# Eight to ten spare bf16 matmuls behind each matrix-vector product of a Householder tridiagonalisation

## The reference

```python
deg = jnp.sum(A, axis=0) + jnp.sum(A, axis=1) - jnp.diagonal(A)
L_norm = d_inv_sqrt[:, None] * (jnp.diag(deg) - A) * d_inv_sqrt[None, :]
_, U = jnp.linalg.eigh(L_norm)
agg = jnp.einsum('mn,bnd->bmd', U.T, features)
h = jax.nn.relu(agg @ W1 + b1)
return jnp.einsum('nm,bmd->bnd', U, h @ W2 + b2)
```

## Time and profile before

| | |
|---|---|
| median of 3 runs | 9881.85 us (9870.64 to 9885.23) |
| profiled execution | 9871.62 us, of it the span of the trace 9869.9 us |
| PE matmul busy | 5128.9 us, 52% |
| VectorE busy | 7105.6 us, 72% |
| ScalarE, GpSimd busy | 18%, 12% |
| steps of the tridiagonalisation | 1022 (x1022 at L483) |
| mean granted TensorE clock | 0.71 of full speed |

### The profile page before, as it was taken

How to read it: one execution, slowest core, us unless ns; L and a number is a source line. 1 busy time by engine, 2 the same in 40 slices (tenths; PEclk the granted TensorE clock), 3 DMA queues, 4 the chain that set the end, 5 groups by cost and what they waited for, 6 DMA issues and landing times. The chain is left out here.

```text
span 9869.9 us, 311313 instructions
## 1 busy us (share of the span) xinstructions
PE 5128.9 (52%) x128994; PEld 3544.3 (36%) x128994; DVE 7105.6 (72%) x33446; ACT 1777.0 (18%) x4691; POOL 1178.6 (12%) x5177
## 2 busy tenths in 40 slices
PE   5675878777777767766654433121111110047856
PEld 2354555555555555554443332010000000033355
DVE  3555666767777776777777778989898989954154
ACT  1432111111111111111111121121111110011054
POOL 0000111111222221222222221000000000000000
PEclk8898999999999777555555555555555555579988
DMA  1000000000000000000000000000000000000000
GB/s 35 1 0 18 4 4 4 4 4 4 4 4 4 4 4 3 4 4 4 4 3 3 3 3 2 0 0 0 0 0 0 0 0 0 0 0 1 17 0 17
DMA packets 24537, 40.99 MB, mean 4 GB/s; under 512 B 2464, under 2 KB 20128, under 8 KB 23200
## 3 DMA queue, kind: packets, MB, share of 16 engines
q1 hardware_dynamic: 23200, 21.70, 0.7%
HBM read 17.50 MB, written 4.19 MB: 2 GB/s over the span
## 5 line engine op out<-in xcount | busy, mean ns | idle before, releaser
L289 PE MATMUL tri_y<-L 128*32 128x256 f32 (+7 forms) x36792 | 2091.7, 366 | 11.9 <-issue 11.6
L289 PEld LDWEIGHTS tri_y<-L 128*32 128x32 f32 x36792 | 1282.2, 132 | 250.7 <-issue 47.9
L1338 PE MATMUL ev_agree<-ev_prod,ev_fold 128*128 128x448 bf16 x520 | 241.5, 568 | 1683.3 <-DVE ev_prod L1461 1666.7
L272 PE MATMUL tri_k<-tri_kp,tri_half 128*32 128x1 f32 x8176 | 270.0, 191 | 1329.4 <-DVE tri_x L472 1329.4
L272 PEld LDWEIGHTS tri_k<-tri_kp,tri_half 128*32 128x32 f32 x8176 | 183.2, 124 | 1695.3 <-DVE tri_x L472 1695.3
L1454 DVE SCALAR_TENSOR_TENSOR ev_seq<-ev_seq,ev_ne2G,ev_u 128x112 f32<-128x112 f32 x2048 | 686.0, 335 | 73.3
L1450 DVE SCALAR_TENSOR_TENSOR ev_u<-ev_x,ev_dG,ev_seq 128x112 f32<-128x112 f32 x2048 | 684.1, 334 | 64.0
L1338 PEld LDWEIGHTS ev_agree<-ev_prod,ev_fold 128*128 128x128 bf16 x520 | 34.6, 111 | 1888.0 <-DVE ev_prod L1461 1867.6
L360 ACT ACTIVATE tri_mu<-tri_ring,tri_tiny 128x1 f32<-128x1 f32 x1022 | 267.1, 261 | 2242.7 <-PE tri_ring L272 2242.7
L272 PE MATMUL tri_ring<-L 128*32 128x32 f32 (+25 forms) x35704 | 639.3, 215 | 0.0
L362 ACT ACTIVATE tri_sM<-tri_half_M,tri_s 128x8 f32<-128x8 f32 (+7 forms) x1022 | 304.3, 298 | 1823.2 <-DVE tri_s L464 1823.2
(11 more groups left out here) (613 smaller groups left out, 12792.4 us busy)
## 6 DMA issues: line engine op xcount, KB each, us to landing
adj<-in_adj_dram SPq DMA_DIRECT2D x12, 1024.0 KB, 8.1
x<-in_x_dram SPq DMA_DIRECT2D x8, 512.0 KB, 7.2
out_dram<-x SPq DMA_DIRECT2D x8, 512.0 KB, 6.6
gcn_w<-in_L_gnn_W_dram SPq DMA_DIRECT2D x2, 128.0 KB, 2.1
spec_w<-in_L_gnn_W_dram SPq DMA_DIRECT2D x2, 64.0 KB, 1.9
dot_wt<-in_L_gnn_W_dram SPq DMA_DIRECT2D x1, 64.0 KB, 1.9
dot_rows<-in_L_gnn_b_lin_dram SPq DMA_DIRECT2D x1, 64.0 KB, 2.7
dot_rows<-in_L_gnn_b_dram SPq DMA_DIRECT2D x1, 64.0 KB, 3.6
```

The source lines that it names most:

```text
L272: last = nc.tensor.matmul(out[32 * g:32 * g + 32, :], lhsT, rhs, start=start, stop=stop)
L289: last = nc.tensor.matmul(y[32 * g:32 * g + 32, 0:T * 32], A[:, b + t, XC:XC + 1].broadcast_to([P, 32]), cols, start=(t == 0), stop=(t == ...
L1338: last = nc.tensor.matmul(agree, fold16[:, :], prod[:, z, h * (GRP // 2):(h + 1) * (GRP // 2), :].rearrange("p s w -> p (s w)"), start=Fal ...
```

## The change

In the blocks with T of 6 or less (the last six), PE gets matmuls behind the last product of each step and ahead of the wait for `kappa_part`: 8 of them in block T = 6 and 10 in each block from T = 5 to T = 1. Each multiplies the bf16 identity by itself (128 x 128 stationary, 128 columns moving) and writes the first 128 columns of ring[3]. Nobody reads them, they wait for nothing and signal nothing. Nothing else is changed.

```diff
                         for t in range(early, T):
                             product(t)
+                        if T <= 6:
+
+                            for _ in range(8 if T == 6 else 10):
+                                nc.tensor.matmul(ring[3][:, 0:P], S["ident16"][:, :], S["ident16"][:, :], start=True, stop=True)
                         pe.wait_ge(kappa_part, r + 1)
                         four(kappa(s), half[:, 0:32], kp[:, :]).then_inc(kappa_ready, 1)
```

## The result

The changed kernel takes 9795.97 us (median of 4, 9786.74 to 9803.36) against 9876.24 us for the kernel before, measured with it (median of 4, 9865.95 to 9885.23). The ratio is 0.9919, 95% interval 0.9901 to 0.9936: 0.8% faster. The forecast was 9792 us, its own range 9755 to 9830 us.

The account below looks back on a forecast made before the run. PE's lower clock costs time in T = 6 to 4, VectorE's chain bounds the rest. 17 + 48 + 22 + 4 = 91 us, less pushed kappas 88 us: median 9792 us, range 9755 to 9830 us.

Parts of the forecast that it names:

- The clock as the lever: Blocks T = 6 to 1: hidden spare matmuls add streaming work and raise PE's clock; 88 us less in all.
- Rival 1: The spare matmuls don't count: every block's clock stays, time 9882 us or up to 15 us more; chance 0.12.
- the strict reading of the rule on continuous work: Half of PE's idle time in each step stays, so by the Trainium skill's rule the change would do nothing.
- The clocks by block: PE clocks after the change in T = 6 to 1: 0.98, 0.93, 0.83, 0.65, 0.5, 0.5.
- T = 5, 4 and 3: Time lost at the lower clock and recovered in these blocks: 48, 22 and 4 us.
- The T = 3 term: T = 3: only kappa's and sigma's latencies gain, 0.05 to 0.10 us a step; a third at upper level, 4 us.
- T = 6: Block T = 6: clock dips in its steps cost about 18 us, nearly all recovered, 17 us.
- T = 2 and 1: Last two blocks: PE's products hide behind VectorE's chain, clocks stay at 0.5, nothing gained.
- Price and cover: A spare matmul takes 0.055 or 0.11 us, hidden in PE's idle time ahead of kappa, 1.09 to 2.03 us a step.
- rival 3: Spare matmuls are as dear as float32 ones, 10 taking 2.1 us at the lower level; 10,025 us, chance 0.14.
- The push of kappa: T = 5 and T = 4 at the lower level: kappa up to 0.15 us later, 2 to 5 us in all.
- Rival 2: Spare matmuls count for more than their columns; all six blocks near 1.00, 150 us less, 9732 us; chance 0.14.

Follow-up runs that it names:

- Experiment 1: Changed kernel with each spare matmul moving one column instead of 128, same number and places; span 9892.9 us.
- experiment 2: Changed kernel with the same spare columns in fewer, wider matmuls (512 and 256 columns); 9796.28 us, ratio 0.9914.
- Experiment 8: Changed kernel with no spare matmuls in T = 6, 12 in T = 5 to 3, none in T = 2 and 1; 9810.68 us, ratio 0.9928.
- experiment 4: Changed kernel without its spare matmuls in T = 2 and 1; 9798.13 us, ratio 0.9916.
- experiment 5: Changed kernel with 8 spare matmuls in T = 6, 12 in T = 5 to 3, none in T = 2 and 1; 9796.93 us, ratio 0.9919.
- experiment 6: Kernel of experiment 4 plus 64 one-column matmuls (128 instructions), once, ahead of the loop of T = 2; span 9785.5 us.
- experiment 7: Changed kernel with 20 spare matmuls instead of 10 in T = 5 to 1; 9825.47 us, ratio 0.9942.
- experiment 3: Changed kernel with spare matmuls using 32 output columns of the array instead of 128, same count and moving columns; span 9798.4 us.
- Experiment 9: Changed kernel with 8 spare matmuls in T = 6, 12 in T = 5 to 3, 16 in T = 2 and 1; 9787.03 us, ratio 0.9904.

## Why the prediction was right, and where it wasn't

**The clock as the lever: right.** Experiment 1 keeps every instruction and takes only the columns away, and the whole gain goes. Rival 1 (they don't count) and the strict reading of the rule on continuous work fell with the clocks of T = 5 to 3. The Trainium skill, page "TensorE: Matmul & The Clock Gate", section "Why this matters for your kernels", asks for TensorE to be kept busy continuously, which read strictly means the idle stretches closed; the traces show 0.92 in T = 5 with 86.4 us of PE idle time left ahead of kappa.

**The clocks by block: right.** Forecast 0.98, 0.93, 0.83, 0.65, 0.5, 0.5; measured 0.97, 0.92, 0.83, 0.67, 0.50, 0.50. Comparing each block's streaming work with the next block's was enough.

**T = 5, 4 and 3: right.** 48, 22 and 4 us forecast; 46.2, 26.9 and 4.9 measured. Without the panel changes it is 43.1, 24.6 and 3.3 us. The 57 steps of T = 4 that went from the lower level to the upper became 0.37 us shorter each, where rows 3 gave 0.35. The T = 3 term rested on an estimate of 0.05 to 0.10 us a step. Over the steps of T = 3, kappa's eight matmuls take 0.243 us at the upper level and 0.286 at the lower, and from the end of L426 (L430 after) to ScalarE's root it is 0.365 against 0.410 us: 0.09 us together. The 28 steps of T = 3 that ran wholly at the upper level took 0.093 us less than the same steps before.

**T = 6: the dips went, and a cost was missing.** 17 us forecast, 2.8 measured in this pair. Each step of the changed kernel can be set against the same step before. The 18 steps that had a dip are 19.3 us shorter, so the 17 us came. The 105 steps that ran wholly at the upper level in both are 10.0 us longer, 9.9 of it in 16 of them. One step has a dip only after (1.5 us), and the panel changes are 5.1 us longer, which the change need not have done: in T = 7, whose code is the same everywhere, one takes anything from 18.1 to 23.4 us. The 16 steps are the pauses, and the prediction named no cost of the instruction stream. The weight loads of the products in T = 6 show them, as a group in the kernel before:

```profile
L289 PEld LDWEIGHTS tri_y<-L 128*32 128x32 f32 x6136 | 212.3, 117 | 22.3 <-issue 1.1
```

and in the changed kernel, with one of the pauses in its timeline:

```profile
L289 PEld LDWEIGHTS tri_y<-L 128*32 128x32 f32 x6136 | 198.6, 112 | 31.5 <-issue 15.5
...
2601.46 0.80 PEld L289 LDWEIGHTS tri_y<-L 128*32 128x32 f32 x23 [0.99 <-issue]
```

1.1 us of idle time for which nothing is waited has become 15.5 us, in pauses of 0.5 to 1 us in the middle of a product, where VectorE waits for y. They come at the same few steps of a panel, though not at all of them in every panel. A step of the changed kernel has 304 PE instructions. Counted so from the panel's start in units of 256 (the first step, which has fewer, like the others), steps 3, 9, 14, 19 and 25 begin 144 to 176 instructions into a unit. In experiment 2 a step has 292, and steps 4, 11, 18 and 25 begin at 132 to 144. In block T = 7, which nobody changed, a step has 320 and the pauses come every 4 steps, 1280 instructions or five whole units, in the kernel before too. So the pauses go with the position of the fetch units in the step. Position isn't all: in T = 6 of the kernel before (288 instructions) steps 5, 13, 21 and 29 begin at 160, and only two of these 16 show a pause. Why one such position stalls and another doesn't (my guess: a whole unit that falls between two waits of PE, so that the next one has no time to arrive) wasn't tried. Experiment 8 suggests that the gain of T = 6 is rather some 9 us than 2.8, but its two executions without spare matmuls differ by 11 us.

**T = 2 and 1: the sign of a small term.** Nothing was forecast there, 5.6 and 1.8 us were lost. The matmuls were hidden as predicted (in T = 2 the steps other than a panel's first took 0.8 us less in sum). The loss of T = 2 is its loop's position, experiments 4 to 6. That of T = 1 is inside what executions differ by: experiments 5 and 6 have 491.3 and 491.0 us there without a spare matmul. The forecast's 88 us came out as 79.4 in the spans (80.3 in the medians) in part by luck, because misses cancelled. Against the 91 us of its blocks: 14 us less in T = 6, 7 in T = 2 and 1 and 2 in T = 5; 5 us more in T = 4, 1 in T = 3, and 6 us from the parts that nothing changed. (Its last addition is off by 2 us: 9784 and 10 are 9794.)

**Price and cover: right.** 0.055 and 0.11 us forecast for a spare matmul, 0.057 and 0.107 measured, so rival 3 (0.21 us) is out. The push of kappa was 0.2 us in the 8 steps of T = 4 that ran at the lower level, where up to 0.15 was allowed for, some 2 us in all. That the cover is no larger than rows 6 say is shown by experiment 7.

**Rival 2: out**, by the clocks and by experiment 3. Its price for T = 3 to 1 at the upper level, 38 us or 0.10 us a step, was right: in experiment 7, 218 steps of these blocks ran wholly at the upper level and took 21.7 us less than the same steps before. The 153 others took 23.7 us more, through pushed kappas, so nothing was left. Experiment 9 got 3.6 us in T = 2.

## What to carry to other kernels

If PE falls to the lower clock in a stage that isn't idle but thin, put hidden spare columns where PE waits for another engine anyway: as many as the wait covers at the lower level and no more. Expect the gain only where the clocked work is on the path (here 46 and 27 us in T = 5 and 4, whose products are on the path at the lower level, and 5 us in T = 3, which VectorE bounds). For the clock, few wide matmuls did as well as many narrow ones, and 32 output columns as well as 128, and in unrolled loops every added instruction also shifts what comes behind it, which can cost as much as a small gain brings.

## What the runs showed of the hardware

- The granted clock didn't depend on how many output columns the spare matmuls use: 32 of 128 output columns gave 0.91, 0.84 and 0.70 in T = 5 to 3, all 128 gave 0.92, 0.83 and 0.67.
- Instructions arrive in packets of 16.4 KB, about 260 instructions each (14,828 in 57). In T = 2 and 1 a loop whose start is shifted by half a packet took 2.1 to 2.7 us more for each jump back, and 128 instructions of padding took it away again (528.3 to 520.1 us, 495.0 to 491.0 us). In T = 4 no such cost showed (13.0 against 13.3 us).
- The latency of small matmuls depended on the clock less than the throughput of spare ones did: eight one-column matmuls 0.286 us at the lower level and 0.243 at the upper, a spare matmul 0.107 and 0.057 us.
